# Making y on quarters of the TensorE array: 64x64 products in place of 128x128 ones

## The reference

```python
y = einsum('bct,bcd->bdt', x, L0_cond_weights[itok])      # 64 x (64 x 64) by (64 x 1024)
base = einsum('bsi,oi->bso', y, W_org)                     # 1024 -> 1024
q = einsum('bi,ki->bk', y.mean(axis=1), Wq)
coeffs = softmax(einsum('bk,ek->be', q, lora_keys) / sqrt(128), axis=-1)
h = einsum('bsi,eir->bser', y, lora_down)                  # 8 experts, rank 64
delta = einsum('be,bser,ero->bso', coeffs, h, lora_up)
out = x + base + delta
```

## Time and profile before

| | |
|---|---|
| median of 3 runs | 708.14 us (708.04 to 709.35) |
| the profiled execution, its time | 708.99 us |
| the profiled execution, its span | 707.2 us |
| PE busy | 699.1 us, 99% |
| DVE busy | 506.1 us, 72% |
| ACT busy | 287.0 us, 41% |
| POOL busy | 127.3 us, 18% |
| PE rows on y (`y_ps`), busy | 59.0 us |

### The profile page before, as it was taken

The page is one execution under the profiler, slowest core; times in us unless marked ns, Lnnn a source line. Parts: engine busy times, 40 slices in busy tenths (PEclk is TensorE's granted clock), DMA queues, the critical chain, the costliest instruction groups (busy, mean ns, idle before and its releaser), DMA issues.

```text
span 707.2 us, 10597 instructions
## 1 busy us (share of the span) xinstructions
PE 699.1 (99%) x3345; PEld 586.2 (83%) x3345; DVE 506.1 (72%) x821; ACT 287.0 (41%) x584; POOL 127.3 (18%) x136
## 2 busy tenths in 40 slices
PE   8999999999999999999999999999999999999997
PEld 7887888888888888888888878888888888888876
DVE  4998776785865865655756997677877777776774
ACT  4566856756758543523624722222211222221120
POOL 3310000000100000000000043323233233323360
PEclk9999999999999999999999999999999999999999
DMA  9993583764844924432444846666566776766732
GB/s 241 312 354 133 150 254 135 217 216 134 261 173 126 276 105 140 129 120 61 164 135 168 332 119 198 210 218 219 203 227 234 238 238 223 238 216 209 269 110 89
DMA packets 97049, 137.80 MB, mean 195 GB/s; under 512 B 14810, under 2 KB 66018, under 8 KB 94178
## 3 DMA queue, kind: packets, MB, share of 16 engines
q1 hardware_dynamic: 96976, 137.12, 59.4%
q10 hardware_dynamic: 18, 0.00, 0.0%
HBM read 81.53 MB, written 55.57 MB: 194 GB/s over the span
## 4 chain that ended last, share of the span: by engine, by line
PE 86%; DVE 7%; issue 4%; DMA 1%; ACT 1%; SPq 0%; DVEq 0%; ACTq 0%
PE x_ps L1476 22%; PE w_ps L1476 17%; PE x_ps L1432 11%; PE h_ps L1398 11%; PE x_ps L1398 11%; PE w_ps L1432 8%; PE y_ps L1357 6%; DMA x_sb<-in_x_dram 1%; DVE tu_l L879 1%; DVE blk L882 1%; DVE ba_l L879 1%; DVE ysum L895 1%; DVE tb_l L879 1%; DVE down_l L879 1%; DVE bs L882 0%
## 5 line engine op out<-in xcount | busy, mean ns | idle before, releaser
L558 POOL TENSOR_TENSOR blk<-blk,blkx 128x512 f32<-128x512 f32 x60 | 94.2, 1572 | 275.1 <-DVE blk L882 204.9
L882 DVE TENSOR_TENSOR blk<-w_ps,blk 128x512 f32<-128x512 f32 x96 | 66.1, 688 | 67.0 <-PE w_ps L1432 31.1
L1476 PE MATMUL x_ps<-tb_h,ba_h 128*128 128x512 f32 x256 | 100.0, 391 | 0.5 <-DVE blk L882 0.3
L1476 PE MATMUL x_ps<-tb_h,ba_l 128*128 128x512 f32 x256 | 99.7, 389 | 0.0
L1476 PE MATMUL x_ps<-tb_l,ba_h 128*128 128x512 f32 x256 | 99.6, 389 | 0.0
L605 ACT ACTIVATE ba_h<-bs 128x512 fp32r<-128x512 f32 x64 | 38.1, 625 | 123.7 <-DVE bs L879 123.7
L1476 PE MATMUL w_ps<-tb_h,ba_h 128*128 128x512 f32 x192 | 74.9, 390 | 0.6 <-DVE ba_l L879 0.6
L1476 PE MATMUL w_ps<-tb_h,ba_l 128*128 128x512 f32 x192 | 74.7, 389 | 0.0
L1476 PE MATMUL w_ps<-tb_l,ba_h 128*128 128x512 f32 x192 | 74.7, 389 | 0.0
L544 POOL COPY cws<-table 64x64 f32 x60 | 20.5, 341 | 284.8 <-PE y_ps L1357 273.8
L605 ACT ACTIVATE ba_h<-yb 128x512 fp32r<-128x512 f32 x48 | 28.4, 621 | 104.3 <-DMA yb<-y_dram 104.3
(11 more groups left out here) (103 smaller groups left out, 1414.4 us busy)
## 6 DMA issues: line engine op xcount, KB each, us to landing
y_dram<-y_full SPq DMA_DIRECT2D x64, 256.0 KB, 3.8
yb<-y_dram SPq DMA_DIRECT2D x32, 512.0 KB, 7.3
out_dram<-blk SPq DMA_DIRECT2D x64, 256.0 KB, 3.8
x_sb<-in_x_dram SPq DMA_DIRECT2D x31, 512.0 KB, 5.1
blkx<-in_x_dram SPq DMA_DIRECT2D x30, 512.0 KB, 6.9
r_dram<-blk SPq DMA_DIRECT2D x56, 256.0 KB, 2.4
blk<-r_dram SPq DMA_DIRECT2D x14, 1024.0 KB, 6.6
t_dram<-st SPq DMA_DIRECT2D x16, 448.0 KB, 5.3
```

Source lines behind the costliest of these rows:

```text
L558: pool.tensor_tensor(blk[p % 3][:, b, :], blk[p % 3][:, b, :], blkx[:, h, n, :], ALU.add).then_inc(x_added, 1)
L882: nc.vector.tensor_tensor(dst, a, b, ALU.add).then_inc(done, 1)
L1476: mm = nc.tensor.matmul(bank, ba[s][n][:, k, :], tb[w][n][:, k, :], start=(first and k == 0 and i == 0), stop=(k == 3 and i == 2), skip_gr ...
```

## The change

From the fifth tile on (n >= 8) `make_y` is replaced by `make_tile(t)`, which makes a whole tile. For each of the 8 chunks it issues four matmuls: for batch b (rows 64b to 64b + 63 of x and of `cws`) and half c of the chunk's 128 inputs (64 columns of x as the stationary operand), the moving operand is the batch's own 64x64 block of `cws`. The result lands on partitions 64c to 64c + 63 of bank `y_ps[:, b]`, so a bank now belongs to a batch and no longer to a half-tile, and each product uses one quarter (64 rows, 64 columns) of the array. The zeros of `cws` are no longer read. `make_tile` waits for both half-tiles of the tile before; `y_done` still goes up by two for a tile, but both times at its end, so `made(n)` is now the tile's last count. `copy_y(n)` reads its four chunks from both banks, 64 columns at a time, and writes them to `y_full` as before.

```diff
-        BEFORE = {6: 0, 3: 1, 5: 2, 7: 4, 8: 6, 9: 3}
+        BEFORE = {6: 0, 3: 1, 5: 2, 7: 4}
 
         def made(n):
-            return FIRST.index(n) + 1 if n < 8 else n + 1
+            return FIRST.index(n) + 1 if n < 8 else n // 2 * 2 + 2
...
+        def y_half(n):
+            r = n % 2
+            return y_ps[:, :, 4 * r * C:4 * (r + 1) * C].rearrange("p b (k d) -> p b k d", d=C)
+
+        def by_batch(half):
+            return half.rearrange("p k (b d) -> p b k d", b=BT)
...
-                copy(y_full[:, n % 8, :, :], y_bank(n).rearrange("p (k n) -> p k n", k=4), y_copied)
+                if n >= 8:
+                    copy(by_batch(y_full[:, n % 8, :, :]), y_half(n), y_copied)
+                else:
+                    copy(y_full[:, n, :, :], y_bank(n).rearrange("p (k n) -> p k n", k=4), y_copied)
...
+            def make_tile(t):
+                wait_for_x(t)
+                if t == 4:
+                    for n in (6, 3):
+                        pe.wait_ge(*copied(n))
+                else:
+                    pe.wait_ge(*copied(2 * t - 1))
+                for k in range(KC):
+                    for b in range(BT):
+                        for c in range(2):
+                            rows64 = slice(b * C, (b + 1) * C)
+                            out64 = slice(c * C, (c + 1) * C)
+                            col = k * P + c * C
+                            mm = nc.tensor.matmul(y_ps[out64, b, k * C:(k + 1) * C], x_sb[rows64, t % 4, col:col + C],
+                                                  cws[rows64, t % 3, b, :, :].rearrange("p h d -> p (h d)"),
+                                                  start=True, stop=True)
+                        if k == KC - 1:
+                            mm.then_inc(y_done, 1)
...
                         if more:
-                            make_y(n + 2 * m)
-                            make_y(n + 2 * m + 1)
+                            make_tile(4 * (q + 1) + m)
```

More of the change, by code:

```diff
@@ L308, in y_bank @@
         def y_bank(n):
-            if n < 8:
-                return (y_ps, w_ps)[n in (2, 4, 5, 7)][:, n not in (0, 6, 2, 5), :]
-            return y_ps[:, n % 2, :]
+            return (y_ps, w_ps)[n in (2, 4, 5, 7)][:, n not in (0, 6, 2, 5), :]
+        def y_half(n):
[3 more added lines that the diff above has]
+            return half.rearrange("p k (b d) -> p b k d", b=BT)
         def down_half(s, n, r):
@@ L1340, in _, with wait_for_x @@
         def _(pe):
[L1341 to L1346, removed]
+            def wait_for_x(t):
+                pe.wait_ge(x_loaded[t % 4], 16 * (t // 4 + 1))
                 if t in (2, 3):
@@ L1350, in make_y @@
                     pe.wait_ge(cw_ready, cw_count(t) + BT)
+            def make_y(n):
+                t, r = n // 2, n % 2
+                wait_for_x(t)
+                if n == 1:
+                    pe.wait_ge(x_rest_loaded, 16)
                 if n in BEFORE:
                     pe.wait_ge(*copied(BEFORE[n]))
-                elif n >= 10:
-                    pe.wait_ge(*copied(n - 2))
                 for k in range(4):
                     col = (4 * r + k) * P
-                    mm = nc.tensor.matmul(y_bank(n)[:, k * P:(k + 1) * P], x_sb[:, i, col:col + P],
+                    mm = nc.tensor.matmul(y_bank(n)[:, k * P:(k + 1) * P], x_sb[:, t, col:col + P],
                                           cws[:, t % 3, :, :, :].rearrange("p b h d -> p (b h d)"),
```

## The result

The changed kernel takes 697.94 us, median of 4 runs (697.35 to 698.45), beside 708.27 us of the kernel before in 4 runs (708.04 to 709.35): a ratio of 0.9849 (0.9837 to 0.9862). It is 10.3 us faster, 1.5%. The prediction said 720.7 us and a range of 711 to 773, slower with a chance of 0.81. The side came out wrong; the rival that happened is "quarters wholly side by side", which had 0.15 and 692 us (686 to 698).

What follows compares the result with a forecast made beforehand. TensorE's own stream was taken to bound the kernel. Per tile 1.92 + 0.32 - 1.79 = +0.45 us, over 28 tiles +12.6 us on 708.14, gave 720.7 us, range 711 to 773.

Steps and rivals of the forecast that it cites:

- quarters wholly side by side: Rival for the y tile: four quarters overlap fully, 1.22 us a tile with switching, -16 us, 692 us; chance 0.15.
- TensorE sets the end: In the rounds PE is busy 48.00 of 48.00 us and waits for nobody, so y tile time reaches the run.
- Loads set the pace of y before: In the old y tile each weight load of 128 columns holds the path 0.11 us, whatever streams behind it.
- The pair of load and matmul: In the new y tile, 64 pairs at 0.03 us each make 1.92 us, against 1.79 before.
- the two ways: Estimates of a y tile: 64 pairs at 0.03 us, 1.92 us; or one 0.056 for each of 32 products, 1.79 us.
- The lower bound: For a y tile: four quarters side by side, each with 16 loads of 0.056 us, 0.90 us.
- The step to quarters and back: Mode switch around each y tile, 56 times: 0.16 us twice, 0.32 us a tile, ends 0.10 and 0.54.
- the cheap transpose: The keys' transpose behind the full-size warm-up, ending 0.16 us after it, usually 0.11: a switch may cost only 0.05 us.
- The wait moved to the front and the later copies: Around each y tile, the earlier wait and the copies at its end cost nothing, covered by the h block.
- DVE could follow: In the side-by-side rival, DVE, busy 34.78 us of 48 in a round, could follow rounds 2.3 us shorter.
- serial loads: Rival for the y tile: loads one after the other, 0.056 us each, +59 us, 767 us; chance 0.26.
- half overlapped: Rival for the y tile: each product pays 0.03 plus 0.056 us, 2.75 us a tile, 744 us; chance 0.15.

Runs made afterwards that it cites:

- row halves: The changed kernel with one product of 64 rows and the full 128 columns per chunk and batch, 16 products a tile: 718.57 us, ratio 1.0135.
- column halves: The changed kernel with two products of all 128 rows and 64 columns per chunk, zeros included, 16 products a tile: 716.85 us, ratio 1.0117.
- turns of whole quarters: The changed kernel with a tile's 32 products reordered: all 8 chunks of one quarter, then the next quarter; 760.91 us, ratio 1.0745.
- double: The changed kernel with seven of the eight chunks of each y tile made twice, same result: 717.21 us in its one execution.
- turns of four chunks: The changed kernel with a tile's 32 products reordered: four chunks (eight trace rows) of one quarter, then four of the next; 736.41 us, ratio 1.0391.
- turns of two chunks: The changed kernel with a tile's 32 products reordered: two chunks of one quarter, then two of the next; 700.31 us, ratio 0.9889.
- halved tile: The changed kernel with y made for only four of the eight chunks, 32 rows a tile where there were 64: 697.49 us, ratio 0.9853.

## Why the prediction was wrong, point by point

- *TensorE sets the end*: right. (That PE waits for nobody in the rounds was not quite so: the trace of before has one wait of 0.3 us on ScalarE's `blk`, in round 0.) The run followed the chain of PE, down to 0.50 us for each tile, as long as VectorE had its work ready.
- *Loads set the pace of y before*: right as far as it went, 0.11 us for each load of 128 columns. The row halves show it again: with only 64 columns to stream the pace stays at 0.111. The column halves add that the 128 streamed columns would have bound at nearly the same pace, 0.109, if it is the stream that sets it there.
- *The pair of load and matmul*: this is the step that failed, the price of 0.03 us for a pair and 1.92 us for a tile. "I take 1.92 us, since the two ways meet there and neither needs the program order to be broken." Both ways rested on the rule that a matmul starts after the one ahead of it, and the first also on pairs that follow one another. In the changed kernel four loads of 0.13 us start within 0.02 us, each 0.002 us ahead of its matmul, and the rows start in an order that is not the program's (the 60th starts 62nd; in turns of whole quarters the 32nd started 35th). A pair adds 0.058 / 4 = 0.0146 us, half of the 0.03 that I took for the shortest. The 0.03 was a distance on one full array, between a load and its own matmul. It bounds one quarter's chain and says nothing of four side by side. The lower bound, 16 x 0.056 = 0.90 us, was the true value (0.93 measured), and it had come from the same row; I gave it 0.15 because it needed pairs faster than any in the trace of before, a trace in which nothing could have been faster.
- *The step to quarters and back*: 0.32 us a tile was taken, 0.16 + 0.21 = 0.37 measured, and it doesn't depend on the tile's length (half, whole and double). Only a size was off there. The row of h at the full array, whose latency of 0.39 stands 0.16 beyond its pace, was the right bound to take; the cheap transpose was not. Its 0.05 compared the ends of two rows of different length; by their starts, 5.16 and 5.37 us, the transpose came 0.10 beyond the usual distance. By the Trainium skill's "TensorEngine Tiling (Array Packing)", Key Properties, a change of mode drains the engine. The trace agrees as far as it goes; its lines stand below this list.
- *The wait moved to the front and the later copies*: nothing, as said; in the rounds PE waits for no copy, and a copy out of two banks still takes 0.60 us.
- *DVE could follow*: half wrong. The rival's text let VectorE follow rounds 2.3 us shorter because it was busy 34.78 of 48. It followed in rounds 1, 5 and 6, and in rounds 2 to 4 it cost 0.65 us each by its order, with 12 us of idle time elsewhere in the round. Round 0, where the prediction had VectorE nearly as the bound, gained 1.7 us less than its four tiles are worth. With -0.50 for a tile and these 3.6 us, the rival's own sum would have been 708.3 - 13.9 + 3.6 = 698.0.
- *The other rivals*: serial loads are real, at 0.058 us each, in the order that puts a quarter's products one behind the other (760.9 us); a time near half overlapped came with turns of four chunks (736.4 us), by another mechanism, the queues. Both were prices of an order that the change doesn't have.

On the change of mode: before, the first load of a tile started while the last matmul of h was just beginning (119.81, its matmul at 120.04):

```profile
119.81 1.98 PEld L1357 LDWEIGHTS y_ps<-cws,x_sb 128*128 128x128 f32 x16
```

In the changed kernel the first load of a tile and the first load of h behind it start only with their own matmuls (117.28 and 118.37):

```profile
117.28 1.02 PEld L1389 LDWEIGHTS y_ps<-cws,x_sb 64*64 64x64 f32 x64 [0.35 <-issue]
118.37 0.19 PEld L1431 LDWEIGHTS x_ps<-yq_h,down_h 128*128 128x128 f32 x1
```

The last row of h still lasts until 117.35 by the trace's modelled end, so how empty the array must be the trace doesn't tell.

Of the start of packed products the Trainium skill says in "TensorE: Matmul & The Clock Gate", Measured speedup vs the span model, that they start some 4 ns apart. Here the first rows of four quarters start 0.0066 us apart with another row of the same quarter between each two, so 0.0033 us a row; in turns of two chunks, with three rows between, they start 0.0134 apart, the same 0.0033. The same page of the Trainium skill says in The mechanism that matmuls start and end strictly in program order. The rule of the prediction that failed says the same of the starts, and the runs differ: in the run with whole quarters in turn the 32nd row starts 35th, and the measurement decides.

## What to carry to other kernels

Where a product's load and its stream are equally wide, as here, splitting it over parts of the array gained only in both directions at once, and only with the quarters in short turns (a product each, or two at the price of 0.15 us a tile; turns of four cost more than they save). With eight chunks a tile the step into the mode and back took 0.37 us of the 0.86 that quarters saved, so it pays to make as many such products in one visit as there are free banks. When a trace of before has no instance of an operation, a shortest distance seen in it is not a floor for another mode of the engine. And when the bounding engine gets shorter, look at the other engines' order ahead of the step it will wait for, not at their busy share.

## What the runs showed of the hardware that was not expected

- Each quarter behaves like a queue of its own, with room for three rows behind the one that starts: the next quarter's first row starts about 0.005 us after the fifth row of a turn of eight, and at once after turns of four. A row can start ahead of rows that stand before it in the program and wait for another quarter: nine of them in turns of two chunks; with whole quarters in turn the 32nd row started 35th. In every kernel here the tile's last row in the program was also the last to start, so a count at its end came last; no run shows that this must be so, and other orders should be checked before a count in the middle is relied on. What the queue looks like inside the engine no run shows.
- On a quarter two rows are 0.058 us apart, on two row halves 0.111, on two column halves 0.109. Whether the load or the stream sets the 0.058 of a quarter no run here tells, since both are half as wide.
- The first row on a quarter that had none running or waiting is followed 0.107 us later by the second, later ones by 0.058 (a tile's start, and each turn of eight).
- After PE had waited 2.3 us in a round of the halved tile, the granted clock stood at 1.2 GHz for 3.2 us, and matmuls of 512 columns came 0.43 us apart and not 0.23. In the profiled execution of the changed kernel, whose waits are 0.5 us at most in the rounds, it stayed at 2.4 GHz. A wait of that length does not always do it (round 3 of the halved tile), and none is needed: in the row halves the clock stood at 1.2 GHz from 25.1 to 28.4 us, in round 0, with PE busy without a gap since 14.07. What set it off there no run shows.
